# Head attention: the weighing of the values two steps back goes ahead of the scores in TensorE's order

## The reference

```python
q = layernorm(x); k = v = ctx_1024
qh = split_heads(q @ Wq + bq)       # 16 heads of 8
kh = split_heads(k @ Wk + bk)
vh = split_heads(v @ Wv + bv)
scores = einsum('bhsd,bhtd->bhst', qh, kh) / sqrt(8)
attn = softmax(scores)              # over 1601 context rows
out = einsum('bhst,bhtd->bhsd', attn, vh)
x = x + out @ Wo + bo
```

## Time and profile before

| | |
|---|---|
| median of 3 runs | 2032.52 us (2031.21 to 2034.72) |
| profiled execution | 2015.73 us, its span 2013.9 us |
| mean granted TensorE clock | 0.947 |
| busy: TensorE, ScalarE, VectorE | 1750.1 us (87%), 1358.7 us (67%), 1036.5 us (51%) |
| busy: weight loads, GpSimd | 1128.2 us (56%), 241.4 us (12%) |

### The profile page before, as it was taken

One profiled execution on the slowest core, in us unless ns is written; L12 is line 12 of the kernel. 1 busy time (PEld: TensorE's weight loads), 2 busy tenths in 40 slices (PEclk: granted clock), 3 DMA queues, 4 the chain that ended last, 5 costly groups with the idle time before them and its releaser, 6 DMA issues. The chain is left out here.

```text
span 2013.9 us, 48671 instructions
## 1 busy us (share of the span) xinstructions
PE 1750.1 (87%) x19832; PEld 1128.2 (56%) x19832; DVE 1036.5 (51%) x2602; ACT 1358.7 (67%) x1600; POOL 241.4 (12%) x155
## 2 busy tenths in 40 slices
PE   3459999999999289999999999999984699999998
PEld 2348998998998044454445454544442355555554
DVE  6984222222222435555555555555524777777773
ACT  1444444444443079999999999999992477776675
POOL 6452000000000300000000000000000021112222
PEclk9769999999999589999999999999996799999999
DMA  8000000000000233333333333333302000000000
GB/s 274 1 14 32 1 1 2 1 1 2 1 1 1 60 76 83 81 81 80 82 81 81 80 81 80 82 79 83 61 8 62 0 6 1 6 5 5 5 5 11
DMA packets 36203, 85.57 MB, mean 42 GB/s; under 512 B 10649, under 2 KB 23330, under 8 KB 35618
## 3 DMA queue, kind: packets, MB, share of 16 engines
q1 hardware_dynamic: 33954, 76.30, 16.1%
q0 software_dynamic: 2048, 6.36, 1.0%
HBM read 30.43 MB, written 2.10 MB: 16 GB/s over the span
## 5 line engine op out<-in xcount | busy, mean ns | idle before, releaser
L1256 ACT ACTIVATE C_probs<-C_ps_s 128x1024 f32<-128x1024 f32 x832 | 772.0, 1076 | 67.2 <-PE C_ps_s L1171 67.0
L1184 PE MATMUL C_ps_o<-C_probs,C_values 128*16 128x256 f32 x6656 | 440.4, 382 | 7.4 <-DVE C_o_t L1402 6.4
L1722 ACT ACTIVATE D_hidden<-D_ps_u,D_b_up 128x1024 f32<-128x1024 f32 x256 | 275.3, 1113 | 147.4 <-PE D_ps_u L1638 147.3
L751 ACT ACTIVATE B_hidden<-B_ps_h,B_b_up 128x512 f32<-128x512 f32 x288 | 194.1, 687 | 189.8 <-PE B_ps_h L679 187.8
L692 PE MATMUL B_ps_e<-B_w_down,B_hidden 128*128 128x128 f32 x2304 | 275.1, 276 | 0.0
L692 PEld LDWEIGHTS B_ps_e<-B_w_down,B_hidden 128*128 128x128 f32 x2304 | 270.3, 192 | 8.4
L1171 PE MATMUL C_ps_s<-C_queries,C_keys 32*128 32x256 f32 x3328 | 212.4, 329 | 58.0 <-ACT C_probs L1256 41.3
L1184 PEld LDWEIGHTS C_ps_o<-C_probs,C_values 128*16 128x16 f32 x6656 | 153.7, 96 | 147.2 <-ACT C_probs L1256 9.8
L1171 PEld LDWEIGHTS C_ps_s<-C_queries,C_keys 32*128 32x128 f32 x3328 | 127.6, 184 | 190.1 <-ACT C_probs L1256 130.9
L846 DVE SCALAR_TENSOR_TENSOR B_acc<-B_ps_e,B_gate,B_acc 128x128 f32<-128x128 f32 x224 | 63.1, 344 | 288.6 <-PE B_ps_e L692 288.6
L1638 PE MATMUL D_ps_u<-D_up_in,D_w_up_r 128*128 128x512 f32 x512 | 186.5, 446 | 2.6 <-ACT D_hidden L1722 1.2
(11 more groups left out here) (270 smaller groups left out, 2018.1 us busy)
## 6 DMA issues: line engine op xcount, KB each, us to landing
C_keys<-C_k_hi SPq DMA_DIRECT2D x128, 200.1 KB, 4.2
C_ctx_t<-ctx_t_dram SPq DMA_DIRECT2D x16, 800.5 KB, 4.4
C_keys<-C_k_lo SPq DMA_DIRECT2D x64, 200.1 KB, 4.1
C_queries<-C_q_hi SPq DMA_DIRECT2D x128, 32.0 KB, 2.3
B_w_up<-L_ffn_w_up_dram SPq DMA_DIRECT2D x1, 2304.0 KB
B_w_down<-L_ffn_w_down_dram SPq DMA_DIRECT2D x1, 2304.0 KB, 19.2
C_queries<-C_q_lo SPq DMA_DIRECT2D x64, 32.0 KB, 2.3
C_queries<-C_blank SPq DMA_DIRECT2D x16, 128.0 KB, 2.8
```

The lines of the kernel that those rows point to most:

```text
L751: nc.scalar.activation(hidden[:, e % HB, c, :], ps_h[c][:], ACT.Gelu, bias=b_up[:, u:u + 1]).then_inc(s_hid, 1)
L1184: m = T.matmul(ps_o[32 * j:32 * j + 2 * DK, g % 2, :], values[:, parity, kt, g * HG + j, :], probs[:, slot(parity, 2 * step + j // 2), j % ...
L1256: nc.scalar.activation(probs[:, slot(parity, n)], ps_s[bank(parity, n)][:], ACT.Exp, scale=SCORE_SCALE1).then_inc(s_exp, 1)
L1722: nc.scalar.activation(hidden[:, u % RING, :, :], ps_u[u % 2][:], ACT.Gelu, bias=b_up[:, u % PAIRS:u % PAIRS + 1]).then_inc(s_hid, 1)
```

## The change

The weighing is moved ahead of the scores within each step. Nothing else is touched: the same matmuls, the same waits on each of them, and the same positions of jobs, `finish` and maxima behind both.

```diff
--- before.py
+++ after.py
@@ -1213,15 +1213,15 @@
                                 pe.wait_ge(s_top_read, TOP_READS + 1)
                             placed(pe, parity, turn)
                             lowered(pe, parity, turn)
+                        if n >= LAG:
+                            weigh(k, parity, n - LAG)
+                        elif not first:
+                            weigh(k - 1, 1 - parity, STEPS - LAG + n)
                         scores(k, parity, n)
                         if first and n == 0:
                             for v in range(BEFORE_SCORES, NJ):
                                 job(0, 0, 0, v, *FIRST_JOBS[v])
                             pe.wait_ge(s_job_done, NJ)
-                        if n >= LAG:
-                            weigh(k, parity, n - LAG)
-                        elif not first:
-                            weigh(k - 1, 1 - parity, STEPS - LAG + n)
                         if n in JOB_AT and not last:
                             if JOB_AT[n] == PREPARED:
                                 pe.wait_ge(s_top_read, TOP_READS * (k + 2) + 1)
```

## The result

The changed kernel takes 2040.68 us (median of 6 runs, 2037.97 to 2046.82) against 2033.62 for the kernel before (6 runs, 2031.21 to 2035.3): 7.1 us more, a ratio of 1.0037 with a 95% interval of 1.0021 to 1.0054. Forecast were 6.6 us more, from a base of 2032.52.

What follows compares the result with a forecast made beforehand. ScalarE's exponentials were taken to bound the stage, with TensorE's order moving only their pauses. The terms 0.8 + 4.8 + 0.6 - 0.5 + 0.9 = 6.6 us, on a median of 2032.52, gave 2039.1 us, range 2036 to 2043.

Steps and rivals of the forecast that it cites:

- ScalarE sets the end; the change can only move its pauses: In stage C, ScalarE's exponentials are 772.0 us busy and 67.2 idle; TensorE's order can win only part of 67 us.
- Length of a step: On TensorE, steps with a job take 1.87 us against 1.86, in some 12 late steps of 14 rounds: +0.8 us.
- Start of a round: Steps 0 to 2: W(0), the round's first weighing, waits for VectorE's reading of old sums; 14 x 0.34 = +4.8 us.
- The pause at n = 15: Around steps 15 to 17, earlier jobs' gain is handed back by weighings: +0.6 us in 14 rounds, -0.5 in the first.
- the first new pause: On ScalarE before unit 30, about 0.8 us: S(15) is behind W(13), which waits for VectorE's reading of ps_o.
- Start of the stage: First steps, TensorE at half clock: two weighings instead of one stand before S(3), +0.9 us (0.6 to 1.4).
- rival 1: No measurable change: VectorE's reading slips in earlier or the step is the short 1.74 us; about 2032 us, chance 0.21.
- rival 2: Faster: at n = 15 the register load and branch ends earlier, so the pause is not paid back; 2026.8 us, chance 0.10.
- rival 3: Much slower: job steps on TensorE grow, by 0.1 us in 17 job steps x 15 rounds; 2058 us, chance 0.09.

Runs made afterwards that it cites:

- e1: Changed kernel, with the two reductions of each round's first key job moved behind VectorE's reading of the old sums: 2037.46 us, ratio 1.0017 to before.
- e2: Changed kernel, with weighing first only in steps 0 to 14 and scores first again in steps 15 to 25: 2028.76 us, ratio 0.9979 to before.
- f2: Kernel before, with the first key job's reductions moved behind VectorE's reading of the old sums: 2036.41 us, ratio 1.0018.
- e4: Changed kernel, with four 128x128 transposes filling TensorE's idle time behind the maxima's branch of step 14: 2038.13 us, ratio 1.0023 to before.

## Why the prediction was right

- *ScalarE sets the end; the change can only move its pauses.* Right: the 7.1 us lie between the exponentials of stage C.
- *Length of a step, +0.8.* The parts were right to 0.01 us: 0.44, 0.46, 0.98, in sum 1.87 to 1.88 against 1.86. Its worth was too small: the stretches outside the two places where the order moves a wait lost 2.6 us. The 0.01 to 0.02 of each late step is a real cost, and halving it for "rounding" was wrong. By the Trainium skill, TensorEngine Tiling (Array Packing), Key Properties, each change of tiling mode drains TensorE, and a step has two of them in either order. The trace agrees within 0.02 us a step; but the prediction's reading of the rule, that the loss would then be 0, does not hold, for these 0.02 us make the 2.6.
- *Start of a round, +4.8.* Right in place, cause and size (5.1), and the cause is shown by e1: taking the reductions out of the way gives back 0.24 of the 0.36 us a round.
- *The pause at n = 15, handed back.* Right, and closer than the 0.0 us of the account shows. With the branch and the falls taken off, the order is worth -0.01 us a round (6.00 to 5.99), where +0.04 was forecast, and -0.6 us in the first round, where -0.5 was. The parts: the first new pause was put at 0.8 and is 0.99 in most rounds, since W(13) takes 1.18 us there and not 0.97 (1113.75 to 1114.93). e2 shows that it is the two weighings that take the gain.
- *Start of the stage, +0.9.* Wrong, it was -0.5. The rows of TensorE, scores of step 1 to scores of step 3:

```profile
730.17 0.80 PE L1171 MATMUL C_ps_s<-C_queries,C_keys 32*128 32x256 f32 x8
...
731.76 1.50 PE L1184 MATMUL C_ps_o<-C_probs,C_values 128*16 128x256 f32 x16
733.19 0.51 PE L1171 MATMUL C_ps_s<-C_queries,C_keys 32*128 32x256 f32 x8
...
735.06 0.51 PE L1171 MATMUL C_ps_s<-C_queries,C_keys 32*128 32x256 f32 x8
```

The second weighing does stand there, but S(3) comes 4.89 us behind S(1) where before it was 5.34. The clock rose earlier: 1.7 us behind the first exponential of step 1, against 4.7 in before. In f2, with scores first, the same stretch is 0.2 us longer than in before, and in e1 1.0 longer than in after, though their edits do not touch it. Over all traces the clock rose 1.7 to 3.9 us behind the first exponential of step 1 in the four kernels that start with the weighing first, and 4.6 to 5.9 in the six that start with the scores first. Units 0 to 6 of the first round take 17.2 to 18.1 us in the four and 17.7 to 17.9 in the six, 17.7 and 17.8 on average. So the second weighing is there, but the earlier clock pays for it; what makes the clock rise earlier is not shown, and single traces differ by more than the term.
- *Not forecast:* the two falls of the clock, +1.8 us, and branches shorter by 0.08 us on average of 15 rounds, -1.2 in sum. Both are in the measured row of units 28 to 34: -0.1 of the order, -0.6 of the first round, +1.8, -1.2 and 0.1 of the last round make the 0.0.
- *The sum.* That 6.6 and 7.1 lie so close is in part luck. The stage's start was 1.4 us less than forecast, the steps 1.8 us more, and the falls and the branches happened to leave 0.6. The mechanism stands without it: the places where something was lost, and the one where nothing was won, are those of the prediction.

The rivals: no gain came from a reading that slips in earlier or from a short step (rival 1), the branch did not end earlier by enough (rival 2, 0.08 us a round, where 0.47 was the turning point), and the step did not grow by 0.1 (rival 3, whose price counts 17 job steps a round where there are 18).

## What to carry to other kernels

Moving work within the order of an engine that has no slack moves waits and not time: ask of each piece what waits for it and what it waits for, and which of these is on the path of the engine that sets the end. Here the jobs deserved to come earlier and the weighing did not; putting the jobs ahead of the weighing gave 12 us (7.3 of it by the order, the rest by shorter branches), and putting the weighing ahead of the scores cost 7 with the same earlier jobs. A pause repeated in every round is worth following back through each engine to the one instruction that frees it. And where one part varies by chance, take it off round by round before comparing two orders: what looked like a spread of 1 us was 6.00 us in every round.

## What the runs showed of the hardware

A register load with a branch on VectorE took 1.1 to 2.3 us over all traces from the end of the operation ahead of it to the semaphore behind the branch, with the same instructions in each round. Most of the spread is the load of the flag into a register, recorded as TENSOR_LOAD, which took 0.30 to 1.27 us; the rest took 0.78 us in most rounds and 1.06 to 1.15 in four or five. TensorE loads the same flag: in e4 the load at 1111.58 took 0.97 us, and the transposes behind the branch start 1.24 us after the scores ahead of it.

```profile
1111.52 0.51 PE L1172 MATMUL C_ps_s<-C_queries,C_keys 32*128 32x256 f32 x8
1113.26 0.63 PE L1237 MATMUL C_ps_p<-ident 128*128 128x128 f32 x4 [1.24 <-issue]
```

The granted clock fell from 1.00 to 0.50 for 3.4 us in the midst of a stage in which TensorE is 92% busy (643 of 700 us in after), behind two idle stretches of 1.54 and 0.43 us; in most rounds with the same stretches it did not. A fall of 3.4 us behind step 14 cost 0.8 to 1.1 us.

VectorE's reading of `ps_o` starts 0.07 us behind the weighing that it waits for, whether VectorE had been free for 0.09 us or, in the last round of before, for 6.6. In e1 and f2, where two waits fall together and one of them is an instruction of its own, it starts 0.14 us behind, in every round. That is half of the 0.18 us a round by which the edit makes f2 slower.
